# A decoder's second cross attention: keys folded into the query weights, softmax by half token tile

## The reference

```python
q = rmsnorm(einsum('bsd,dhe->bshe', x, Wq), gq)      # over e, 64 numbers
k = rmsnorm(einsum('bsd,dhe->bshe', ctx, Wk), gk)
v = einsum('bsd,dhe->bshe', ctx, Wv)
scores = einsum('bqhe,bkhe->bhqk', q, k) / sqrt(64)
attn = softmax(scores)                               # over the 77 context rows
out = einsum('bqhe,hed->bqd', einsum('bhqk,bkhe->bqhe', attn, v), Wo) + bo
```

## Time and profile before

| | us |
|---|---|
| median of 3 runs | 1205.21 (1202.03 to 1206.45) |
| the profiled execution, its own time | 1207.17 |
| its span in the trace | 1205.5 |
| PE busy | 894.1 (74%) |
| DVE busy | 871.1 (72%) |
| ACT busy | 661.3 (55%) |
| POOL busy | 256.1 (21%) |
| mean granted clock of PE | 0.858 |

### The profile page before, as it was taken

One profiled execution on the slowest core, in us unless ns is written; L12 is line 12 of the kernel. 1 busy time (PEld: TensorE's weight loads), 2 busy tenths in 40 slices (PEclk: granted clock), 3 DMA queues, 4 the chain that ended last, 5 costly groups with the idle time before them and its releaser, 6 DMA issues. The chain is left out here.

```text
span 1205.5 us, 12085 instructions
## 1 busy us (share of the span) xinstructions
PE 894.1 (74%) x3656; PEld 499.5 (41%) x3656; DVE 871.1 (72%) x1703; ACT 661.3 (55%) x1829; POOL 256.1 (21%) x153
## 2 busy tenths in 40 slices
PE   2561478998989589898815248599898976898893
PEld 2450335554366334344414124455435643344432
DVE  1268646886389589999716875587846967999993
ACT  1413369992435285785712053999352435686691
POOL 1011106884070100000000200288515201000000
PEclk9865587998979799999957558699997997999997
DMA  8100012330000000000010000133100000000000
GB/s 217 35 0 1 0 40 59 93 94 0 1 1 1 1 0 1 0 1 1 1 50 1 0 1 5 58 97 90 35 1 1 1 1 1 1 0 1 1 0 18
DMA packets 26814, 27.41 MB, mean 23 GB/s; under 512 B 7172, under 2 KB 17146, under 8 KB 26746
## 3 DMA queue, kind: packets, MB, share of 16 engines
q1 hardware_dynamic: 24776, 24.63, 7.2%
q10 hardware_dynamic: 1970, 1.97, 0.6%
HBM read 25.28 MB, written 1.31 MB: 22 GB/s over the span
## 5 line engine op out<-in xcount | busy, mean ns | idle before, releaser
L1489 POOL TENSOR_TENSOR rs<-ve,minus_half 128x4 f32<-128x4 f32 (+2 forms) x60 | 101.7, 1702 | 816.0 <-DVE ve L1119 686.8
L877 PE MATMUL ps<-mem,ident 128*128 128x512 f32 x512 | 234.3, 607 | 27.7 <-DVE mem L1457 26.9
L909 ACT ACTIVATE mem<-ps 77x512 f32<-77x512 f32 (+7 forms) x172 | 103.6, 605 | 241.7 <-PE ps L818 61.1
L1079 ACT ACTIVATE mem<-mem 128x32 f32<-128x32 f32 x1024 | 217.8, 312 | 0.0
L1302 DVE TENSOR_TENSOR_SCAN mem<-mem,ps 128x1024 f32<-128x1024 f32 x64 | 146.0, 2285 | 45.2 <-PE ps L722 45.2
L1504 POOL TENSOR_TENSOR mem<-mem 128x1024 f32<-128x1024 f32 x64 | 150.8, 2360 | 116.7 <-DVE mem L1302 116.6
L1457 DVE SCALAR_TENSOR_TENSOR mem<-mem 128x1024 f32<-128x1024 f32 x128 | 159.2, 1279 | 13.3 <-ACT mem L1079 11.8
L877 PEld LDWEIGHTS ps<-mem,ident 128*128 128x128 f32 x512 | 95.3, 192 | 165.7 <-issue 95.3
L729 PE MATMUL ps<-mem,ident 128*128 128x512 f32 x256 | 121.7, 602 | 0.0
L1449 DVE TENSOR_TENSOR mem<-mem 128x1024 f32<-128x1024 f32 x96 | 113.0, 1218 | 0.3
L1008 ACT ACTIVATE mem<-mem 128x256 f32<-128x256 f32 x256 | 105.2, 493 | 0.1
(11 more groups left out here) (219 smaller groups left out, 1229.4 us busy)
## 6 DMA issues: line engine op xcount, KB each, us to landing
mem<-bc_rows SPq DMA_DIRECT2D x64, 256.0 KB, 3.2
x<-in_x_dram SPq DMA_DIRECT2D x4, 256.0 KB, 3.7
out_dram<-x SPq DMA_DIRECT2D x4, 256.0 KB, 2.3
mask<-in_mask_BxSxS_ik_dram SPq DMA_DIRECT2D x4, 154.0 KB, 3.5
mem<-n_L_ffn_expert_down_dram SPq DMA_DIRECT2D x1, 512.0 KB
mem<-in_L_xattn_Wo_dram SPq DMA_DIRECT2D x1, 512.0 KB
mem<-in_L_xattn_Wv_dram ACTq DMA_DIRECT2D x1, 512.0 KB
a_q<-in_L_xattn_Wq_dram SPq DMA_DIRECT2D x1, 512.0 KB, 4.7
```

The lines of the kernel that those rows point to most:

```text
L877: mm = pe.matmul(ps[:, j, :], ident[:], WH[s][:, h % WB, j * 512:(j + 1) * 512], start=(h == 0), stop=(h == PH - 1), skip_group_check=True)
L909: ins = nc.scalar.activation(to, of, ACT.Copy, **kw)
L1079: ins = nc.scalar.activation(SVA[s][:, n % 2, i * NK:(i + 1) * NK], sims[:, 1, h, :], ACT.Identity, bias=sims[:, 0, h, i:i + 1])
L1489: nc.gpsimd.tensor_tensor(RS[s][0:rows, i * n:(i + 1) * n], VE[s][0:rows, i * n:(i + 1) * n], minus_half[0:rows, 0:n], ALU.pow)\
```

## The change

In the preparation, PE also turns Wq (`a_qT`), after waiting for the late loads, and ACT copies it; the 17 memsets of `pair_pick` go, two memsets of the padded context `CTP` (128x384) come.

A new generator `memory` is merged into the scan by stage numbers. It stands at 5 + NS and behind on PE: keys at 21, their transposes at 21.9, the scan's output projection at 22, then at 22.2 to 22.8 the folding of keys and Wq (`KW`, for each head 128 x 77) and the values, now laid out in ten chunks of 128 of the 1232 rows (head, context row), by 25 matmuls of 128 columns. On DVE it stands at 21.3 and 21.8, between the scan's y and its residual (22).

In cross1, the queries themselves serve only for their mean square (projection by token tile, squares on ACT, sums on DVE, power on POOL). Scores are x times `KW`, for a half tile u (128 tokens, 8 heads): two matmuls of 308 columns. DVE takes the maximum and multiplies it by minus the scale; ACT does one exponential for each head, with scale, bias and a sum as accumulator output; DVE takes the reciprocal; POOL multiplies. PE turns chunks of 128 weights, DVE copies them, and PE multiplies them with the value chunks so that tokens x d comes out; the last copy and the turn back go.

```diff
+                pe.wait_ge(p_late, ALL_LATE)
+                for j in range(HP):
+                    mm = pe.transpose(PS[0][:, j // 4, (j % 4) * P:(j % 4 + 1) * P], a_q[:, j * P:(j + 1) * P],
+                                      ident[:])
+                mm.then_inc(p_pe, 1)
...
+                def memory(s):
+                    ps = PS[s]
+                    yield 5 + NS
+                    w.next(G("scan_done", s))
+                    for j in range(2):
+                        pe.matmul(ps[0:C, 2 + j, :], CTP[s][:, P:P + C], a_k[:, j * 512:(j + 1) * 512],
+                                  start=True, stop=True).then_inc(G("k_ready", s), 1)
+                    yield 5.9 + NS
+                    w.next(G("kn_ready", s))
...
+                    for half in range(2):
+                        yield 6.2 + 0.2 * half + NS
...
+                        for j in range(4 * half, 4 * half + 4):
+                            for a in range(2):
+                                mm = pe.matmul(ps[:, 2 + a, j % 4 * C:(j % 4 + 1) * C],
+                                               a_qT[a * E:(a + 1) * E, j, :], KT[s][a * E:(a + 1) * E, j, :],
+                                               start=True, stop=True)
+                        mm.then_inc(G("k_ready", s), 1)
+                    for n, (c0, c1) in enumerate(GROUPS):
+                        yield 6.6 + 0.1 * n + NS
+                        if n >= 1:
+                            w.next(G("v_sb", s))
+                        for i in range(c0, c1):
+                            rows = chunk_rows(i)
+                            heads = [h for h in range(H) if h * C < i * P + rows and (h + 1) * C > i * P]
+                            for h in heads:
+                                at = P + i * P - h * C
+                                mm = pe.matmul(ps[0:rows, 1, (i - c0) * P:(i - c0 + 1) * P],
+                                               CTP[s][:, at:at + rows], a_vo[:, h, :],
+                                               start=(h == heads[0]), stop=(h == heads[-1]))
+                        mm.then_inc(G("v_ready", s), 1)
...
+                    for k in range(NB):
+                        yield 1 + k
...
+                        for j in range(2):
+                            mm = pe.matmul(ps[:, k % 2 * 2 + j, :], XT[s][:, k * P:(k + 1) * P],
+                                           a_q[:, j * 512:(j + 1) * 512], start=True, stop=True)
+                        mm.then_inc(G("aq_ready", s), 1)
...
+                        if u == 0:
+                            w.next(G("qsq_ready", s), 2)
+                        else:
+                            w.next(G("p_ready", s))
+                        for a in range(2):
+                            h = 8 * g + 4 * a
+                            mm = pe.matmul(ps[:, a, 0:4 * C], XT[s][:, k * P:(k + 1) * P],
+                                           KW[s][:, h:h + 4, :].rearrange("p a b -> p (a b)"), start=True, stop=True)
...
+                    yield 10
+                    scores(0)
+                    due = None
+                    for u in range(2 * NB):
+                        if u + 1 < 2 * NB:
+                            yield 14 + 4 * u
+                            scores(u + 1)
+                        for n, (c0, c1) in enumerate(GROUPS_OF[u % 2]):
+                            yield 15 + 4 * u + n
+                            weights_turned(u // 2, c0, c1)
+                            if due:
+                                attended(*due)
+                            due = (u // 2, c0, c1)
...
+                        for i in range(8):
+                            h = 8 * g + i
+                            ins = nc.scalar.activation(SC[s][:, k % 2, h, :],
+                                                       ps[:, i // 4, i % 4 * C:(i % 4 + 1) * C], ACT.Exp,
+                                                       scale=RS[s][:, k * H + h:k * H + h + 1],
+                                                       bias=NM[s][:, i:i + 1], accum_out=SM[s][:, u % 2, i:i + 1])
+                        ins.then_inc(G("p_ready", s), 1)
...
+                    yield 11
+                    maxima(0)
+                    for u in range(2 * NB):
+                        yield 13 + 4 * u
                         w.next(G("p_ready", s))
...
+                        nc.vector.reciprocal(RD[s][:, u % 2], SM[s][:, u % 2]).then_inc(G("rd_ready", s), 1)
+                        if u + 1 < 2 * NB:
+                            yield 15 + 4 * u
+                            maxima(u + 1)
+                        for n, (c0, c1) in enumerate(GROUPS_OF[u % 2]):
+                            yield 15.5 + 4 * u + n
+                            weights(u // 2, c0, c1)
...
+                    for k in range(NB):
+                        yield 401.8 + k
+                        rsqrt(s, P, H, k)
+                    for u in range(2 * NB):
+                        yield 413.5 + 4 * u
+                        w.next(sg["rd_ready"][s])
+                        p = SC[s][:, u // 2 % 2, u % 2 * 8:u % 2 * 8 + 8, :]
+                        nc.gpsimd.tensor_tensor(p, p, spread(RD[s][:, u % 2], 2, C), ALU.mult)\
+                            .then_inc(sg["pn_ready"][s], 1)
```

More of the change, by code:

```diff
@@ L518, in in_turn, with merged @@
                 stage[s] = next(runs[s], None)
+        def merged(*runs):
+            stage = [next(r, None) for r in runs]
+            while any(n is not None for n in stage):
+                n, i = min((n, i) for i, n in enumerate(stage) if n is not None)
+                yield n
+                stage[i] = next(runs[i], None)
         def sublayers(phases):
@@ L740, in cross1, with scan_memory @@
+                def scan_memory(s):
+                    yield from merged(scan(s), memory(s))
                 def cross1(s):
@@ new lines, in scan, with memory @@
+                        yield 3.5 + n
+                        if n >= 2:
+                            w.next(G("dbu_done", s))
+                        for k in range(NB):
+                            ins = nc.scalar.activation(DZ[s][:, n % 2, k, :], DUT[s][:, k, :], ACT.Identity,
+                                                       scale=BT[s][:, k, n:n + 1])
+                        ins.then_inc(G("dz_ready", s), 1)
+                def memory(s):
+                    ps = PS[s]
+                    yield 5.1 + NS
+                    for j in range(2):
+                        w.next(G("k_ready", s))
+                        nc.scalar.activation(KQ[s][:].rearrange("p a b -> p (a b)")[:, j * 512:(j + 1) * 512],
+                                             ps[0:C, 2 + j, :], ACT.Square).then_inc(G("ksq_ready", s), 1)
+                    yield 6 + NS
+                    w.next(G("k_ready", s))
+                    copy(KT[s][:].rearrange("p (a b) c -> p a (b c)", a=2), ps[:, 2:4, 0:4 * C],
+                         G("kT_ready", s), scale=a_g[:, 0:1])
+                    for half in range(2):
+                        yield 6.3 + 0.2 * half + NS
+                        w.next(G("k_ready", s))
+                        copy(KW[s][:, 8 * half:8 * half + 8, :].rearrange("p (j a) c -> p a j c", a=2),
+                             ps[:, 2:4, 0:4 * C].rearrange("p a (j c) -> p a j c", c=C), G("m_sb", s))
+                    for n, (c0, c1) in enumerate(GROUPS):
+                        yield 6.65 + 0.1 * n + NS
+                        w.next(G("v_ready", s))
+                        copy(VW[s][:, c0:c1, :].rearrange("p a b -> p (a b)"), ps[:, 1, 0:(c1 - c0) * P],
+                             G("v_sb", s))
@@ L1026, in cross1 @@
-                    yield 2
-                    turned(s, KT[s][:].rearrange("p (a b) c -> p a (b c)", a=2), ps[:, 1:3, 0:4 * C],
-                           "kT_ready", scale=a_g[:, 0:1])
-                    for j in range(HP):
-                        yield 3.2 + j
-                        w.next(G("aq_sb", s))
-                        nc.scalar.activation(QSQ[s][:, j, :], AQ[s][:, j, :], ACT.Square)\
+                    for k in range(NB):
+                        yield 1.5 + k
+                        w.next(G("aq_ready", s))
+                        if k >= 2:
+                            w.next(G("ssq_done", s))
+                        nc.scalar.activation(QSQ[s][:, k % 2].rearrange("p (a b) c -> p a (b c)", a=2),
+                                             ps[:, k % 2 * 2:k % 2 * 2 + 2, :], ACT.Square)\
@@ L1376, in staged @@
-                    def staged(stage, steps):
-                        yield stage
-                        for n in steps:
-                            yield stage + n
-                    yield from staged(19, logits(0))
-                    for j in range(HP):
-                        if j + 1 < HP:
-                            yield from staged(20 + 3 * j, logits(j + 1))
-                        yield from staged(21 + 3 * j, probabilities(j))
-                    yield 50
```

(1 more changed line is left out.)

397 lines of the change are left out of this document (149 added, 248 removed).

## The result

The changed kernel took 1210.1 us (median of 20 runs, 1205.16 to 1216.56) against 1204.51 (20 runs, 1201.34 to 1210.75) beside it: ratio 1.005, 95% interval 1.0032 to 1.0069. So in this comparison it is slower by 5.6 us, where 12.5 were forecast: the sign holds, the size is under half. The traces can't show it either, as the profiled executions were a short one of the changed kernel (1205.55 us, 4.5 under its median) and a long one of the kernel before (1207.17, 2.7 over the median here). Span of the changed kernel's trace: 1203.8 us.

A forecast was written before the change was run, and what follows sets the result against it. DVE was taken to bound the softmax and PE the query projection, both held by chains after the change. 0.9 + 2 x (-4.3 + 3.3 + 6.8) = +12.5 us on 1207.17 gave 1219.7, 1217 in medians; range 1188 to 1231.

The forecast's parts named there:

- Step 1: Preparation: eight added turns at the low clock before the last matmuls, ACT's copy following in line; about +0.9 us, once.
- Steps 2 and 3: Scan's tail and queries: PE idles for the key chain, then low clock, but first exponential comes earlier; -4.3 us an iteration.
- Step 4: Softmax half tiles: exponentials at 0.41 us plus 1.3 us hand-over make a 7.9 us cycle, before 7.35; +3.3 us an iteration.
- Step 5: Softmax: pauses after even half tiles drop PE's clock, making scores late in odd cycles; +6.8 us an iteration.
- The clock holds: Rival, softmax: half-idle cycles don't drop PE's clock, so its term is nothing; -1.1 us, 1204, no change; chance 0.26.
- Cheaper exponentials: Rival, softmax on ACT: an exponential costs 0.33 us, the read hidden in the next start; 1190.5 us; chance 0.24.
- Much slower: Rival, softmax: exponentials 0.45 us or more, low clock through whole cycle pairs; 1225 us; within 0.50 for forecast and beyond.

The follow-up runs named there:

- values_first: Changed kernel with PE doing the scan's output projection and the value matmuls (with ACT's copies) ahead of the keys' turn: 1188.9 us, 0.9846 of the kernel before.
- keys_late: Changed kernel with PE turning the keys behind the scan's output projection instead of ahead of it: 1207.28 us, 0.9997 of the kernel before.
- combo: Changed kernel with projection and values ahead of the keys' turn, lanes staggered half a cycle, and four POOL powers behind products: 1165.52 us, 0.9656 of the kernel before.
- bare_chain: Changed kernel with four POOL powers moved behind products, maxima in PSUM, and small matmuls filling PE's softmax pauses: 1196.12 us, 0.9918 of the kernel before.
- nosum: Changed kernel without the exponentials' accumulator output, reciprocals taken of ones (result wrong): 1186.24 us, 0.9831 of the kernel before.
- powers: Changed kernel with four of POOL's eight powers moved behind the products of half tiles 1 and 3: 1205.81 us, 1.0005 of the kernel before.
- warm: Changed kernel with small matmuls, overwritten later, filling PE's pauses in the softmax: 1205.46 us, 1.0001 of the kernel before.
- again2: Changed kernel measured once more without an edit: 1204.2 us, 0.9994 of the kernel before.

## Why the prediction was wrong in size, and its sign not borne out

**Step 1, the preparation.** +0.9 us was forecast for eight turns "at the low clock". The window in these rows says 1.00; the eight turns took 1.91 us there and 1.04 in the earlier trace rows, and the trace of the changed kernel grants 0.50 from 31.4 to 33.3 us, where the same turns ran. The added turns moved the last matmuls of the preparation by 0.3 us.

**Steps 2 and 3, the tail: right in kind, 2.3 us too dear.** The key chain came as written: lane 0's keys turn at 288.20 - 272.12 = +16.1 us (forecast 290.5 - 274.40 = +16.1), lane 1's at +18.9 (+19.0), the projection behind them. The low clock cost the forecast 3.0: 2.5 in the projection (6.22 us for 3.73 in values_first) and 0.5 in the key turns (1.29 for 0.75 in keys_late). The rest of PE's work was a little cheaper: values 11.3 for 12.0 from start to start, folding 3.9 for 4.1, the projection at full clock 3.7 for 4.1. PE was at the cross attention at +41.3 for +42.9, and the first exponential at +60.1 for +62.4: -6.6 us against the kernel before for the forecast -4.3. values_first shows that this order costs 11 us of PE's time an iteration; it alone regains 19.5 of the 44 us of "combo".

**Step 4, the chain: right in kind, 2.3 us too dear.** 0.392 us an exponential (0.30 + 0.09) for 0.41 (0.32 + 0.09), hand-over 1.34 for 1.3, POOL's product 1.22 for 1.45: from first exponential to residual bare_chain shows 65.7 us for 68.0, so +1.0 for the forecast +3.3.
The Trainium skill ("ScalarE: Activation LUTs", What ACT_TABLE_LOAD costs) led to an estimate of 0.34 before the accumulator's read; nosum shows 0.30, so the trace is below it, and the read's 0.09 is as forecast.

**Step 5, the clock: this is the step that failed.** "+6.8 us" for PE's clock in an iteration was 1.8 at the start, twice 1.5 between and 2 in the tail. The clock did fall in the cycles of odd half tiles. But from first exponential to residual all disturbances together are 71.5 - 65.7 = 5.8 us (against bare_chain), and in the first iteration they split so:
- PE's clock, 2.4: the fifth cycle 9.25 and the seventh 8.44, each against 7.60 and 0.09 of hold, and 0.1 in the tail. In the second iteration it is 0.8 + 1.0 + 1.3 = 3.1.
- POOL's queue, 1.6: the second cycle, 9.42 against 7.61 and 0.24 of hold. The forecast had 1.8 of clock at this place; "powers" shows that it was the queue. I had set that at nothing, "PE is not on the path there"; it is, since DVE's next maxima wait for scores that PE does behind the turns and products (L824 at 345.67).
- The hold of DVE's scale operation by POOL's product, 1.8: three times 0.45, 0.24 and twice 0.09. No step had it.

The parts depend on each other: taking the clock alone away would give 1.7 of its 2.4, since the hold then fills the fifth and seventh cycle ("warm": 8.05 and 8.04). So a wrong split came near a right sum, and that was luck; by itself the clock term was two to four times what the traces show.
The Trainium skill ("SBUF — State Buffer", Who interferes with whom) has the rule that I passed over: a VectorE instruction with two inputs in SBUF contends with a GpSimd instruction that reads SBUF, over shared ports that it calls an exclusive lock. The trace agrees: 0.62 us, ending with POOL's, and 0.17 with one input in PSUM.

**The sum.** An iteration was forecast at -4.3 + 3.3 + 6.8 = +5.8; the residual moved by -6.6 + 1.0 + 5.8 = +0.2: 2.3 less from the tail, 2.3 from the chain, 1.0 from the disturbances. So most of the missing size is in the two steps whose mechanism was right. Twice 5.6 is 11 us too much in the two stages. Of the +5.6 measured, the stages then explain nothing (265.4 for 266.4), and the sign is no success of the sum. In the rest of the profile I find the preparation's 0.3 us, and 1.8 us more from the last norm statistics to the end (216.2 for 214.4 before, but 214.4 in "again2"). Where the rest comes from, and why two later measurements found no difference, stays open: stages that the change doesn't touch vary by as much between executions of one kernel.

**The rivals.** *The clock holds* came nearest in time (1204), for another reason: the clock fell, the disturbances cost 5.8 us an iteration, and other terms came out lower. *Cheaper exponentials* was priced on the right mechanism: at 0.30, nosum's cycles are 6.7 us and the stage runs 2 x 9.3 us shorter. The read does not hide behind the next start, though: it costs 0.09 us each time. *Much slower* did not occur.

## What to carry to other kernels

When work is moved to leave an engine half idle, look for what it waits on in strict order: a chain of small operations (here sum, power, product for the keys) in front of work that needs none of it costs its whole length, and filling the pause with independent work gains far more than shortening it. In a chain with several small disturbances, removing one at a time shows little, since a lost stall can reappear in the next limit, here PE's low clock or another hold; remove them together once to learn what they are worth. Two lanes in step leave the shared bottleneck idle at each hand-over, and half a cycle of stagger fills it.

## What was not expected of the hardware

- A POOL multiply of 128x616 holds a DVE operation of 128x8 with two SBUF inputs until it ends: 0.62 us for 0.17. With one input in PSUM the 32 operations average 166 ns instead of 290, and staggered lanes avoid the meeting too (167).
- The accumulator's read follows each ACTIVATE 0.30 us after its start and delays the next by 0.09 us.
- PE at the low clock over 8 us (0.50) took 7.12 us for 64 records of 77 columns that took 3.92 at a clock of 1.00; the projection's 32 records took 3.73 us behind busy PE and 6.22, at a mean clock of 0.59, behind the pauses of 5.81 and 1.58.
- The profile's duration of an exponential grows within a run of 16 from 0.41 to 0.47 us while the starts stay 0.392 apart; starts, not durations, price a stream of them.
